# Three row copies of VectorE stay, the fourth of each group is made by ScalarE and GpSimd

## What is computed

```python
dots = einsum('bhid,bhjd->bhij', q, k) * SCALE          # 16 heads, 16 memory keys + the tokens
dots = einsum('bhij,hk->bkij', dots, pre_proj)          # heads mixed
dots = where(causal, -inf, dots)
thresh = top_k(dots, 64)[0][..., -1:]                   # the 64th largest score of each row
dots = where(dots < thresh, -inf, dots)
attn = softmax(dots, axis=-1)
out = einsum('bhij,bhjd->bhid', attn, v)
```

## Time and profile before

| | |
|---|---|
| median of 3 executions | 3034.04 us (3031.94 to 3041.01) |
| profiled execution, own time | 3029.58 us |
| its span, first to last instruction | 3027.1 us |
| VectorE (DVE) busy | 2415.8 us, 80% |
| TensorE (PE) busy | 2302.1 us, 76%; mean granted clock 0.859 |
| ScalarE (ACT) busy | 1414.6 us, 47% |
| GpSimd (POOL) busy | 5.2 us |

### The profile page before, as it was taken

The page is one execution under the profiler, slowest core; times in us unless marked ns, Lnnn a source line. Parts: engine busy times, 40 slices in busy tenths (PEclk is TensorE's granted clock), DMA queues, the critical chain, the costliest instruction groups (busy, mean ns, idle before and its releaser), DMA issues.

```text
span 3027.1 us, 34365 instructions
## 1 busy us (share of the span) xinstructions
PE 2302.1 (76%) x10182; PEld 1328.8 (44%) x10182; DVE 2415.8 (80%) x9392; ACT 1414.6 (47%) x2143; POOL 5.2 (0%) x43
## 2 busy tenths in 40 slices
PE   6696545657767757778888888988984888884897
PEld 3554323333434424444444444544542545442564
DVE  2506688889888988989899999999998988884445
ACT  1121223444445435555565666666663666652221
POOL 0000000000000000000000000000000000000000
PEclk7798667777878878899998999999997999987898
DMA  2000000000000000000000000000000000001000
GB/s 59 1 0 1 1 1 1 1 1 1 2 1 1 1 1 1 1 1 1 1 1 1 1 1 1 1 1 1 1 1 1 1 1 1 1 1 49 1 1 14
DMA packets 15509, 12.20 MB, mean 4 GB/s; under 512 B 6892, under 2 KB 13686, under 8 KB 15222
## 3 DMA queue, kind: packets, MB, share of 16 engines
q1 hardware_dynamic: 11184, 6.82, 0.9%
q10 hardware_dynamic: 4038, 2.37, 0.3%
HBM read 8.14 MB, written 1.05 MB: 3 GB/s over the span
## 4 chain that ended last, share of the span: by engine, by line
DVE 53%; PE 30%; ACT 8%; issue 7%; DVEq 2%; ACTq 0%
DVE cand L1106 13%; DVE R L1155 7%; DVE r L1157 7%; PE bank L823 6%; PE bank L791 6%; PE bank L903 4%; DVE W L1136 4%; DVE F L1176 4%; DVE W L1135 4%; ACT R L543 4%; PE bank L807 3%; ACT R L536 3%; PE bank L911 2%; DVE WP L1170 2%; PE bank L808 1%
## 5 line engine op out<-in xcount | busy, mean ns | idle before, releaser
L823 PE MATMUL bank<-WP,Y 128*128 128x512 f32 x1088 | 685.4, 718 | 152.0 <-ACT WP L550 151.2
L807 PE MATMUL bank<-ident,R 128*128 128x128 f32 x2176 | 524.0, 315 | 248.8 <-ACT R L543 246.6
L1106 DVE MAX8 cand<-R 128x8 f32<-128x12 f32 (+15 forms) x4096 | 642.6, 226 | 5.3 <-ACT R L521 4.2
L791 PE MATMUL bank<-hT,qT 128*128 128x512 f32 (+3 forms) x1280 | 533.1, 555 | 37.3 <-ACT R L521 22.2
L807 PEld LDWEIGHTS bank<-ident,R 128*128 128x128 f32 x2176 | 346.2, 159 | 465.6 <-issue 214.7
L550 ACT ACTIVATE WP<-bank 128x512 f32<-128x512 f32 x544 | 320.8, 594 | 369.8 <-PE bank L808 368.6
L808 PE MATMUL bank<-nidentb,F 128*128 128x128 bf16 x2176 | 466.3, 240 | 0.0
L536 ACT ACTIVATE R<-R,cutb 128x144 f32<-128x144 f32 (+15 forms) x256 | 310.2, 1212 | 294.1 <-DVEq L1148 292.5
L521 ACT ACTIVATE R<-bank 128x1024 f32<-128x1024 f32 (+7 forms) x384 | 290.5, 774 | 278.6 <-PE bank L791 168.3
L1155 DVE SCALAR_TENSOR_TENSOR R<-R,r 128x144 f32<-128x144 f32 (+15 forms) x256 | 350.3, 1368 | 9.2 <-DVE r L1154 0.2
L543 ACT ACTIVATE R<-R,negm 128x144 f32<-128x144 f32 (+15 forms) x256 | 289.8, 1205 | 123.9 <-DVEq L1254 123.7
(11 more groups left out here) (225 smaller groups left out, 2164.1 us busy)
## 6 DMA issues: line engine op xcount, KB each, us to landing
R<-in_L_attn_Wkv ACTq DMA_DIRECT2D x2, 512.0 KB, 8.0
R<-in_L_ffn_gate_w SPq DMA_DIRECT2D x1, 1024.0 KB, 7.7
R<-in_L_ffn_up_w SPq DMA_DIRECT2D x1, 1024.0 KB, 10.3
out<-X SPq DMA_DIRECT2D x1, 1024.0 KB, 5.1
R<-in_L_attn_Wq ACTq DMA_DIRECT2D x1, 512.0 KB, 6.1
WP<-in_L_attn_Wo ACTq DMA_DIRECT2D x1, 512.0 KB, 10.5
R<-in_L_ffn_wi SPq DMA_DIRECT2D x1, 256.0 KB
R<-in_L_ffn_wo SPq DMA_DIRECT2D x1, 256.0 KB
```

The source lines that it names most:

```text
L791: last = pe.matmul(to, qT[:, k % 2, i, :], hT[:, a:b], start=True, stop=b < n, skip_group_check=True)
L807: pe.transpose(to[:, P * i:P * i + P], S[:, k % NS, i, blk], ident[:, :])
L823: pe.matmul(bank[6], Y[:, j, :], PT[:, (blocks_before(k) + j) % 4, :], start=(j == 0), stop=(j == k // 4))\
L1106: mark(dve.max(cand[:, :, c, i], lists(S[:, k % NS, i, 0:n], n, c)))
```

## The change

For the last unit of each group (`i = GU - 1 = 3`), the copy without the scores above the pivot is no longer made by VectorE. ScalarE computes `relu(BIG * score + cutb)` into `A[:, 0]` right after its fourth count: zero up to the pivot, and a huge number above. GpSimd computes `score - A[:, 0]` into `A[:, 0]`. VectorE waits for that and takes its MAX8 from `A[:, 0]`. There are 64 instructions fewer on VectorE, 64 more on ScalarE and 64 more on GpSimd. Since `A[:, 0]` is now read, the first count of a group waits for the eighths of the group before (`s_eight`).

```diff
+        s_over, s_below = sem("s_over"), sem("s_below")
...
+            for k in range(NG):
+                n = wide(k // 4)
+                pool.wait_ge(s_over, k + 1)
+                pool.tensor_tensor(A[:, 0, 0:n], S[:, k % NS, GU - 1, 0:n], A[:, 0, 0:n], ALU.subtract).then_inc(s_below, 1)
...
                 if u:
                     act.wait_ge(s_cnt, u)
+                if i == 0 and k:
+
+                    act.wait_ge(s_eight, u)
                 act.wait_ge(s_cut, k + 1)
...
+            def excess(k):
+
+                n, i = wide(k // 4), GU - 1
+                act.wait_ge(s_cnt, GU * k + GU)
+                act.activation(A[:, 0, 0:n], S[:, k % NS, i, 0:n], ACT.Relu, bias=cutb[:, k % 2, i:i + 1], scale=BIG_)\
+                    .then_inc(s_over, 1)
...
                         count_above(p, i)
+                        if i == GU - 1:
+                            excess(p)
                         for j in turns[3 + i:4 + i]:
                             drain_turn(p - 1, j)
...
                 if i == 0:
                     link(dve.tensor_scalar(r9[:, :, 0], cutb[:, k % 2, :], -1.0 / BIG_, None, ALU.mult))
+                if i == GU - 1:
+                    dve.wait_ge(s_below, k + 1)
+                    dve.max(r9[:, i, 1:9], A[:, 0, 0:n]).then_inc(s_eight, 1)
+                    dve.wait_ge(s_eight, u + 1)
+                    return
```

## The result

The changed kernel takes 3106.95 us (median of 4, 3099.65 to 3111.59) against 3034.38 us before (3031.94 to 3041.01): a ratio of 1.0233, 95% interval 1.0206 to 1.026, or +73 us. The forecast was 3084 us in a range of 3045 to 3130. The profiled execution took 3104.38 us, its span is 3102.6 us, 75.5 us longer than that of before.

What follows compares the result with a forecast made beforehand. VectorE was taken to bound the groups: 88 us less work and 134 us more waiting give +46 us, ScalarE's extra pass +4, so +50 us and 3084 us on the median, with an 8-in-10 range of 3045 to 3130.

Steps and rivals of the forecast that it cites:

- VectorE bounds the groups: Between `cutb` and the masks, a microsecond on VectorE is one in the span, except at the widest rows.
- Removed, 87.6 us: 64 of VectorE's 256 copies go, at 1.368 us on average: 87.6 us less work.
- The hand-offs: Relu to subtract and subtract to MAX8, each passing between engines: 0.15 us each, 0.30 a group.
- E, the relu: ScalarE's added pass behind the fourth count: 0.72 us at 528 columns, 2.00 at 2064, 1.2 on average.
- G, the subtract: GpSimd's subtract ahead of the new MAX8: 0.10 us plus 2.23 ns a column, 4.7 us at 2064.
- Rivals A and B: Other rates of GpSimd's subtract: A, 1.49 ns a column, 3034 us, chance 0.12; B, 3.36 ns, 3162 us, 0.06.
- The first 44 groups: Sampled at widths 528, 1040 and 1168: each group longer by 0.18, 1.19 and 0.29 us.
- C, GpSimd and VectorE shut each other out: Rival: the subtract can't start before VectorE's third MAX8 is over; 3122 us, chance 0.10.
- ScalarE's extra pass: 64 relu passes, some 77 us on ScalarE, delay TensorE's turned blocks in the widest groups: +4 us.
- d: How much later a group's fourth MAX8 starts than before: 0.18 to 2.93 us a group, +46 us in all.

Runs made afterwards that it cites:

- the relu alone: Kernel before plus ScalarE's relu pass behind the fourth count, its result unused, VectorE keeping all four copies: 3086.08 us, ratio 1.0165.
- the last kernel: The change with the relu ahead of the counts, in groups 0 to 43 only; groups 44 to 63 as before: 3011.16 us, ratio 0.9925 to the kernel before.

## Why the prediction was right, and where it was off

- **VectorE bounds the groups.** Right in the first 44 groups: they are 19.6 us longer with the wait for the subtract, the relu alone, which leaves VectorE its copies, doesn't change them, and 21 us less copying in the last kernel makes them 23 us shorter. Wrong in the wide groups: the relu alone, with all 256 copies on VectorE, makes them as long as the change does, and there the masks wait 72.7 us for TensorE, against 25.6 us before. VectorE's own account (64 us ahead of L1175 and 9 us at the masks) gives the 73 us only because VectorE waits for whatever is last.
- **Removed, 87.6 us.** Right: 88 us less busy.
- **The hand-offs.** 0.08 and about 0.11 us where 0.15 was taken twice, so 0.1 us a group too much.
- **E, the relu.** 1.215 us on average, as forecast.
- **G, the subtract.** 4.55 us at 2064 columns, 1.30 at 528, 2.39 at 1040, against 4.70, 1.28 and 2.42. Scaling the cast by the number of streams gave 2.23 ns a column, and 2.11 was measured. That it came so close is luck in part: it rests on two short instructions of 98 and 287 ns, and the first isn't the shortest on GpSimd, where others of one column take 89 ns. Rivals A and B, other rates, are out.
- **The first 44 groups.** The three samples for them gave 3.6 + 14.3 + 12 x 0.29 = 21.4 us; measured 19.6, and +22 us as a kernel of its own. At 784 to 1040 columns the wait does what the step said.
- **C, GpSimd and VectorE shut each other out.** Not in this kernel, whose copies keep 1368 ns, because the subtract starts when the third copy is over, as the prediction worked out for 1040 columns, and runs beside MAX8. But the lock is real, for copies. It was weighed only as a cost on top of the change; it is also the reason why an earlier subtract gains little.
- **The step that failed is "ScalarE's extra pass", the term of +4 us.** For groups 44 to 62 the copies' d (8 x 0.29, 8 x 1.38, 3 x 2.93) and this term gave some 26 us, and 44.5 us were measured; the relu alone makes 43.6. The step set the pass against ScalarE's idle time and against the d that the sum already held, and let only the four widths from 1680 on pay. What the runs showed instead: the pass stands where TensorE has two turned blocks of room, so TensorE runs dry behind it and the blocks come later by the whole pass, 1.6 to 2.0 us, in all 20 groups from 1552 columns on; and in 8 of them (9 in the change) the clock falls too, and the stretch is 3.3 to 3.7 us longer. The bill comes from where the pass stands: 10 us behind the blocks, 23 in halves, 51 as it is. With that, the wait for the subtract adds next to nothing in the wide groups; what it would cost there by itself was not measured.
- **The forecast was 23 us too low.** Against the profile of before, 18.5 us are missing in groups 44 to 62 and 1.9 us behind the last group's `cutb` (4.8 measured, 2.9 forecast); that too is ScalarE's pass, since the relu alone has the same 4.8 us. The first groups took 1.8 us less than forecast. The remaining 4 us lie ahead of group 0 and in the spread between executions.
- **Luck in the range.** The time lies inside it, but its upper end was set for C and for a slower subtract, and neither came. What filled it was the term of +4 us, which by the 20 wide groups should have been some 24.

## What to carry to other kernels

When a side engine takes over a step, add up its whole chain from the point that releases it, and compare it with the moment the result is due; here VectorE's wait for it was longer than the copy that it replaced at every width, 0.7 against 0.37 us at 144 columns and 5.1 against 2.37 us at 2064, though ScalarE was busy 48% of the time and GpSimd 5%. Ask of an engine that is half idle not only how much more it does, but who waits for the instruction behind. And look at what work moved from VectorE to GpSimd runs beside: here the subtract left MAX8, with one SBUF input, alone, and made the copies, with two, wait.

## What was unexpected of the hardware

- A GpSimd subtract and a VectorE copy with two SBUF inputs exclude each other for whole instructions: a copy of 2.37 us took 4.23, a subtract of 4.55 us took 6.56. Of 87.6 us of copies moved away, 67.6 came back as longer copies, and with two passes on GpSimd 90.6.
- TensorE, idle for 2.72 us behind blocks at full clock, came back in one group at a granted clock of 0.54 to 0.61 and was at 1.00 again some 3.5 us later; in another group of the same width it came back at full clock after the same 2.72 us.
- On GpSimd a compare against a per-row value, with one input, takes 4.19 us on average, longer than the two-input subtract's 2.77 in the same kernel. It always started within 0.4 us of a copy on VectorE, so part of it may be waiting; its own rate isn't shown.
